# A two-branch attention: VectorE's share of the square moved before the second tile's absolute value, all lags one slot shorter

## The reference, cut to what matters

```python
S = jnp.einsum('bhnd,bhmd->bhnm', Q, K) / dh ** 0.5
W_tau = jax.nn.softmax(S, axis=-1)
W_sigma = 1.0 / ((1.0 + jnp.abs(S) / b_) ** 2 + t_ ** 2)
W_sigma = W_sigma / W_sigma.sum(axis=-1, keepdims=True)
tau = jnp.einsum('bhnm,bhmd->bhnd', W_tau, V)
sigma = jnp.einsum('bhnm,bhmd->bhnd', W_sigma, V)
f = 0.5 * tau + 0.5 * sigma
```

## Time and profile before

| | before |
|---|---|
| time, median of 3 runs | 2975.97 us (2975.95 to 2976.5) |
| time of the profiled execution | 2972.06 us |
| its span | 2970.4 us |
| busy: PE, DVE, ACT, POOL | 2445.4, 2491.1, 2234.4, 1992.1 us |
| granted TensorE clock, mean | 0.936 of full |

### The profile page before, as it was taken

The page is one execution under the profiler, slowest core; times in us unless marked ns, Lnnn a source line. Parts: engine busy times, 40 slices in busy tenths (PEclk is TensorE's granted clock), DMA queues, the critical chain, the costliest instruction groups (busy, mean ns, idle before and its releaser), DMA issues. The chain is left out here.

```text
span 2970.4 us, 60006 instructions
## 1 busy us (share of the span) xinstructions
PE 2445.4 (82%) x18487; PEld 1018.8 (34%) x18614; DVE 2491.1 (84%) x3983; ACT 2234.4 (75%) x2441; POOL 1992.1 (67%) x1236
## 2 busy tenths in 40 slices
PE   3755999998577994689999999999999999983898
PEld 2642333333474662122222222222222222222566
DVE  4666888885577657799999999999999999996765
ACT  4532777777364543499999999999999999993554
POOL 4510222222453651499999999999999999994465
PEclk9976999999687997699999999999999999997799
DMA  3222111000120002000000000000000000000000
GB/s 116 70 64 87 30 29 29 28 27 11 45 79 5 1 0 86 22 15 14 16 15 14 14 16 15 14 14 16 15 14 14 16 15 14 14 5 0 1 12 18
DMA packets 93504, 76.58 MB, mean 26 GB/s; under 512 B 32480, under 2 KB 73960, under 8 KB 93264
## 3 DMA queue, kind: packets, MB, share of 16 engines
q1 hardware_dynamic: 89104, 66.36, 7.8%
q0 software_dynamic: 4288, 8.82, 0.9%
HBM read 47.77 MB, written 24.42 MB: 24 GB/s over the span
## 5 line engine op out<-in xcount | busy, mean ns | idle before, releaser
L1761 POOL TENSOR_TENSOR a_sg<-a_sg,all_f0w 128x1632 f32<-128x1632 f32 x256 | 940.7, 3675 | 21.3
L1967 DVE TENSOR_REDUCE a_mx<-a_pm 128x1 f32<-128x1024 f32 x512 | 618.3, 1208 | 23.2 <-PE a_pm L1813 23.2
L1978 DVE TENSOR_SCALAR a_sg<-a_pa 128x1024 int32<-128x1024 int32 x512 | 614.9, 1201 | 3.8 <-PE a_pa L1813 3.8
L1894 ACT ACTIVATE a_pt<-a_pb 128x1024 f32<-128x1024 f32 x512 | 532.4, 1040 | 55.0 <-PE a_pb L1813 53.4
L1831 PE MATMUL a_po<-a_pt,a_Vh 128*32 128x512 f32 x2048 | 538.4, 604 | 15.0 <-ACT a_osb L1913 11.4
L1831 PE MATMUL a_po<-a_sg,a_Vh 128*32 128x512 f32 x2048 | 538.3, 604 | 0.0
L1758 POOL TENSOR_SCALAR all_f0w<-a_sg,a_parh 128x1632 f32<-128x1632 f32 x256 | 506.7, 1979 | 37.4 <-DVE a_sg L1978 37.3
L1903 ACT ACTIVATE a_sg<-a_sg,a_parh 128x2048 f32<-128x2048 f32 x256 | 517.0, 2020 | 0.0
L1907 ACT ACTIVATE a_sg<-a_sg 128x2048 f32<-128x2048 f32 x256 | 496.0, 1937 | 0.0
L1581 ACT ACTIVATE a_pt<-a_ring 128x1024 f32<-128x1024 f32 (+2 forms) x384 | 313.7, 846 | 164.4 <-PE a_ring L1508 161.2
L1653 DVE TENSOR_REDUCE a_mx<-a_ring 128x2 f32<-128x1024 f32 (+3 forms) x384 | 359.2, 955 | 85.1 <-PE a_ring L1491 66.1
(11 more groups left out here) (265 smaller groups left out, 4457.9 us busy)
## 6 DMA issues: line engine op xcount, KB each, us to landing
all_Q<-q_parts SPq DMA_DIRECT2D x256, 48.0 KB
all_K<-k_parts SPq DMA_DIRECT2D x256, 48.0 KB
k_parts<-p_parts SPq DMA_DIRECT2D x16, 384.0 KB, 2.6
e_recs<-routed_rows SPq DMA_DIRECT2D x70, 64.5 KB, 1.9
n_xn<-expert_rows SPq DMA_DIRECT2D x16, 256.0 KB, 4.2
all_Q<-a_rows SPq DMA_DIRECT2D x256, 2.0 KB
q_parts<-p_parts SPq DMA_DIRECT2D x16, 192.0 KB, 2.3
q_parts<-p_parts SPq DMA_DIRECT2D x8, 384.0 KB, 2.6
```

Source lines behind the costliest of these rows:

```text
L1761: nc.gpsimd.tensor_tensor(buf[:, :, 0:CUT], buf[:, :, 0:CUT], sums, ALU.mult)\
L1894: nc.scalar.activation(pt[(j - LT) % 4][:, i, :], pb[:], ACT.Exp, scale=SC)\
L1967: nc.vector.tensor_reduce(mx[:, (j // PER) % 2, t:t + 1], pm[:], AX.X, ALU.max)\
L1978: nc.vector.tensor_scalar(sg[(j - LS) % 4][:, i, :].bitcast(I32), pa[:].bitcast(I32), SIGN_OFF, None, ALU.bitwise_and).then_inc(abs_done, 1)
```

## The change

Four things change, all in `attend_both`:

- The DVE square works on columns 0 to 415 of the first tile alone (`CUT` = 13 * 1024 / 32 = 416), where it had 208 columns of each tile. GpSimd's share is what is left of the two tiles seen as one row of 2048: 1632 columns. Both shares are as large as before.
- The DVE square needs the abs of the first tile only, and stands between the second tile's maximum and the second tile's abs.
- The turning of the maxima moves from the second to the first half of an iteration, and both parts of `negated` run in that same iteration. `output` and the turning of `osb` are spread differently: the add into F (L1957 in the changed kernel) now stands just before the DVE square.
- All lags fall by one: `LS`, `LT`, `LE`, `LP` from 5, 7, 7, 8 to 4, 6, 6, 7. The distances between the square, the reciprocal and the weighing stay the same; the distance from the maxima to the softmax's scores falls by a slot.

```diff
--- before.py
+++ after.py
@@ -1673,9 +1673,9 @@
     SLOTS = HEADS * TT // 2
     PER = TT // 2
     UNROLL = PER * RING
-    LS, LT, LE, LP = 5, 7, 7, 8
+    LS, LT, LE, LP = 4, 6, 6, 7
     SC = DH ** -0.5
-    CUT = 51 * T // 64
+    CUT = 13 * T // 32
     WIDE = TT * (DH + 1)
     with ExitStack() as ctx:
         m = Mem(nc, ctx, tag)
@@ -1686,8 +1686,8 @@
         rows = m.sb("rows", [TT, MAX_PARTS, P], BF16)
         pt = [m.sb(f"pt{r}", [P, 2, T]) for r in range(4)]
         sg = [m.sb(f"sg{r}", [P, 2, T]) for r in range(4)]
-        shifted = [scratch[:, 4 * CUT * r:4 * CUT * (r + 1)].bitcast(F32).rearrange("p (i n) -> p i n", i=2)
-                   for r in range(2)]
+        REST = 2 * T - CUT
+        shifted = [scratch[:, 2 * REST * r:2 * REST * (r + 1)].bitcast(F32) for r in range(2)]
         osb = m.sb("osb", [P, CH])
         rz = m.sb("rz", [P, 4, 4])
         fw = m.sb("fw", [P, 4, 4, DH])
@@ -1730,7 +1730,7 @@
             with eng.Fori(1, SLOTS // UNROLL) as it:
                 for j in range(UNROLL):
                     body(it, j)
-            for j in range(LP + 4):
+            for j in range(LP + 5):
                 body(SLOTS // UNROLL, j)
 
         def some(x, least=1):
@@ -1747,7 +1747,8 @@
                     s = at(it, j, LS)
                     if s is None:
                         return
-                    buf, sums = sg[(j - LS) % 4], shifted[(j - LS) % 2]
+                    buf = sg[(j - LS) % 4][:].rearrange("p i n -> p (i n)")[:, CUT:]
+                    sums = shifted[(j - LS) % 2]
                     if some(s, 2):
                         pool.wait_ge(sq_pool, s - 1)
                     if (j - LS) % PER == 0:
@@ -1755,10 +1756,10 @@
                     pool.wait_ge(abs_done, 2 * s + 2)
                     pool.nop(nofuse=True)
                     b2 = parh[:, ring(j, LS), 0:1]
-                    nc.gpsimd.tensor_scalar(sums, buf[:, :, 0:CUT], b2, 1.0, ALU.add, ALU.mult)\
+                    nc.gpsimd.tensor_scalar(sums, buf, b2, 1.0, ALU.add, ALU.mult)\
                         .then_inc(shift_done, 1)
                     pool.wait_ge(shift_done, s + 1)
-                    nc.gpsimd.tensor_tensor(buf[:, :, 0:CUT], buf[:, :, 0:CUT], sums, ALU.mult)\
+                    nc.gpsimd.tensor_tensor(buf, buf, sums, ALU.mult)\
                         .then_inc(sq_pool, 1)
 
                 slots(pool, body)
@@ -1853,7 +1854,7 @@
                             if some(2 * ss + i):
                                 pe.wait_ge(abs_done, 2 * ss + i)
                             scores(pa, K[rs], Q[rs], 2 * ((j - LS) % PER) + i, 96, abs_mm)
-                        if i == 1 and j % PER == 0 and at(it, j, 1) is not None:
+                        if i == 0 and j % PER == 0 and at(it, j, 1) is not None:
 
                             h = head(it, j, 1)
                             pe.wait_ge(max_red, TT * h + TT)
@@ -1864,19 +1865,19 @@
                         sp_ = at(it, j, LP + 1 - i)
                         if sp_ is not None:
                             weigh(it, j, sp_, 1 - i)
-                    if (j - LP - 2) % PER == PER - 1 and at(it, j, LP + 2) is not None:
-
-                        h = head(it, j, LP + 2)
-                        pe.wait_ge(o_sb, h + 1)
-                        if isinstance(h, int) and h + 3 > HEADS:
-                            pe.wait_ge(rows_sb, HEADS)
-                            pe.wait_ge(f_done, h)
-                        else:
-                            pe.wait_ge(rows_sb, h + 3)
-                        for c in range(4):
-                            last = nc.tensor.transpose(ptr[:, c * P:(c + 1) * P], osb[:, c * P:(c + 1) * P],
-                                                       ident[:])
-                        last.then_inc(o_turned, 1)
+                        if i == 0 and (j - LP - 3) % PER == PER - 1 and at(it, j, LP + 3) is not None:
+
+                            h = head(it, j, LP + 3)
+                            pe.wait_ge(o_sb, h + 1)
+                            if isinstance(h, int) and h + 3 > HEADS:
+                                pe.wait_ge(rows_sb, HEADS)
+                                pe.wait_ge(f_done, h)
+                            else:
+                                pe.wait_ge(rows_sb, h + 3)
+                            for c in range(4):
+                                last = nc.tensor.transpose(ptr[:, c * P:(c + 1) * P], osb[:, c * P:(c + 1) * P],
+                                                           ident[:])
+                            last.then_inc(o_turned, 1)
 
                 slots(pe, body)
 
@@ -1967,26 +1968,24 @@
                             nc.vector.tensor_reduce(mx[:, (j // PER) % 2, t:t + 1], pm[:], AX.X, ALU.max)\
                                 .then_inc(max_red, 1)
                         if i == 0:
-                            negated(it, j, 1, 2)
-                            output(it, j, 0, LP + 3)
+                            output(it, j, 1, LP + 4)
                         else:
-                            output(it, j, 1, LP + 3)
+                            output(it, j, 2, LP + 4)
+                        if i == 1 and ss is not None:
+                            share = sg[(j - LS) % 4][:, 0, 0:CUT]
+                            dve.wait_ge(abs_done, 2 * ss + 1)
+                            if (j - LS) % PER == 0:
+                                dve.wait_ge(head_in[ring(j, LS)], HEAD_LOADS * rounds(it, j, LS))
+                            nc.vector.scalar_tensor_tensor(share, share, parh[:, ring(j, LS), 0:1], share,
+                                                           ALU.add, ALU.mult).then_inc(sq_dve, 1)
                         if ss is not None:
                             dve.wait_ge(abs_mm, 2 * ss + i + 1)
                             if some(ss, 4):
                                 dve.wait_ge(pv_done, 2 * (ss - 4) + i + 1)
                             nc.vector.tensor_scalar(sg[(j - LS) % 4][:, i, :].bitcast(I32), pa[:].bitcast(I32),
                                                     SIGN_OFF, None, ALU.bitwise_and).then_inc(abs_done, 1)
-                    if ss is not None:
-                        buf = sg[(j - LS) % 4]
-                        dve.wait_ge(abs_done, 2 * ss + 2)
-                        if (j - LS) % PER == 0:
-                            dve.wait_ge(head_in[ring(j, LS)], HEAD_LOADS * rounds(it, j, LS))
-                        nc.vector.scalar_tensor_tensor(buf[:, :, CUT:T], buf[:, :, CUT:T],
-                                                       parh[:, ring(j, LS), 0:1], buf[:, :, CUT:T],
-                                                       ALU.add, ALU.mult).then_inc(sq_dve, 1)
-                    negated(it, j, 0, 1)
-                    output(it, j, 2, LP + 3)
+                        negated(it, j, i, 1)
+                    output(it, j, 0, LP + 3)
 
                 slots(dve, body)
         m.clear_sems()
```

## The result

| | before | after |
|---|---|---|
| time, median of 5 runs | 2975.95 us (2971.5 to 2976.5) | 3341.33 us (3338.93 to 3342.76) |
| span of the profiled execution | 2970.4 us | 3337.2 us |
| busy: PE, DVE, ACT, POOL | 2445.4, 2491.1, 2234.4, 1992.1 us | 2560.4, 2778.0, 2259.7, 1904.1 us |
| granted TensorE clock, mean | 0.936 | 0.903 |

The ratio is 1.123, with a 95% interval of 1.1215 to 1.1245. The change makes the kernel 12% slower; 3342 us was forecast. The medians in this document are those of fast runs; one run of e7, 3260.27 us at a mean clock of 0.73, is left out.

A forecast was written before the change was run, and what follows sets the result against it. The prediction took GpSimd, running back to back at 5.70 us a slot, to bound the second attention. 359.6 + 13 - 4.7 - 2 = +366 us on 2972.06 gave 3338, as a median 3342 us; range 3300 to 3440, at 80%.

The forecast's parts named there:

- The lock: Second attention: GpSimd's multiply keeps DVE's square out, which ends some 0.45 us after it; a square keeps GpSimd's shift out.
- The closed cycle: Second attention: square waits for multiply, GpSimd then for the second abs; 7.11 us a slot for 5.70, 359.6 us more.
- The add ahead of the square: Add into F also waits for the multiply, delaying the square by up to 0.2 us in one slot of four: 13 us.
- The fill: Start of the second attention: shorter lags leave out one slot of maxima alone, -4.7 us.
- The last slots: Last four slots lack maxima, so the square may slip in ahead of the multiply: -2 us, within 0 to -5.
- The sum: All terms together: 359.6 + 13 - 4.7 - 2 = +366 us on the profiled execution's 2972.06.
- TensorE's clock: Second attention: TensorE, needing 5.14 us a slot, 72% of 7.16, was left at its granted clock of 1.00.
- Rival 3: TensorE's clock falls in the attention's longer gaps; for a third of it 265 us more, 3600 us; 5%.
- Rivals 1 and 2: DVE runs a slot ahead: 2971 us (6%), or 2958 us if square and shift don't exclude each other (4%).

The follow-up runs named there:

- e7: e1 with DVE's share of the square raised from 416 to 512 of 2048 columns; 2959.62 us, ratio 0.9946 to the kernel before.
- e4: Changed kernel, its order kept, with DVE's square and add into F each reading one of their two inputs from PSUM; 2951.49 us, ratio 0.992.
- e5: Changed kernel with GpSimd's multiply replaced by a second shift, so each GpSimd instruction reads one SBUF tensor; 2949.75 us in one run.
- e3: Kernel before with the change's shares and the DVE square ahead of the second abs; lags, turning and add as before; 3334.68 us, ratio 1.1208.
- e2: e1 with the add into F ahead of the second abs in one slot of four; 3046.54 us, ratio 1.0236.
- e1: Changed kernel with the DVE square put back behind the second abs and the add into F at the slot's end; 2968.59 us, ratio 0.9977.
- e8: Changed kernel with GpSimd waiting in the very first slot for the abs of two slots instead of one; 3340.34 us, ratio 1.123.

## Why the prediction was right

- *The lock.* Shown by e4, with e5 for the shift. The multiply keeps the square out. Whatever else the order costs doesn't reach the time: with the lock gone GpSimd still waits for an abs now and then (31.5 us in the 800), but ACT sets the pace.
- *The closed cycle.* The term was 7.11 us a slot; three slots in four take 7.13 us in the timeline, and e3 with the order alone has 7.13 on the mean. Its parts: the multiply's end to the abs 0.37 (2013.92 to 2014.29), abs 1.21, 0.17 to the shift, shift 1.62 for the 1.60 chosen between 1.50 and 1.97, hand-over 0.09, multiply 3.65. That some 0.35 us of the shift before (the prediction took 0.4) was DVE's square, and not its own work, shows in its median, now 1625 ns for 1970.
- *The add ahead of the square.* 13 us were forecast, 0.2 us a head. The slot with the add:

```profile
2001.23 1.62 POOL L1759 TENSOR_SCALAR all_f0w<-a_sg,a_parh 128x1632 f32<-128x1632 f32 x1 [1.76 <-DVE a_sg L1985]
...
2004.67 2.00 DVE L1957 TENSOR_TENSOR all_XNT<-a_fw 128x64 f32 x1
...
2006.59 0.64 DVE L1979 SCALAR_TENSOR_TENSOR a_sg<-a_sg,a_parh 128x416 f32<-128x416 f32 x1
...
2008.54 1.63 POOL L1759 TENSOR_SCALAR all_f0w<-a_sg,a_parh 128x1632 f32<-128x1632 f32 x1 [1.96 <-DVE a_sg L1985]
```

  It is 7.31 us long, 0.18 more than the others. e2 shows what the prediction left out: the same add would have cost 78 us in a kernel that is otherwise in the good order.
- *The fill.* -4.7 us were forecast. From the first maximum to the first shift it is 4.2 us less in the changed kernel and 4.8 us less in e1.
- *The last slots.* -2 us were forecast and none were won there. Without maxima a square begins 0.46 us after a multiply has begun (3022.86 against 3022.40) and takes 3.65 us. This term was wrong, within its bounds of 0 to -5.
- *The sum.* The cycle and the add were put at 359.6 + 13 = 372.6 us, and the shifts' starts show 373.1. That the totals then agree within 1 us (366 forecast, 366.8 between the spans) is in part luck: the 2 us of the last slots were not won, and 2.5 us came from what was in no term (the stage's earlier start 1.35, the last shift 0.35, the end 0.8).
- *TensorE's clock.* It was left at 1.00 and fell to 0.92 on the mean of the stage (row at the end): the step failed, the 74% of the earlier trace rows was no guide. Rival 3's price did not come with it, though. DVE waits 57 us for maxima's scores in the 1100 us above, and the time comes out of the square's wait:

```profile
2024.50 3.64 POOL L1762 TENSOR_TENSOR a_sg<-a_sg,all_f0w 128x1632 f32<-128x1632 f32 x1
...
2026.31 1.23 DVE L1968 TENSOR_REDUCE a_mx<-a_pm 128x1 f32<-128x1024 f32 x1 [1.24 <-PE a_pm L1814]
...
2027.45 1.14 DVE L1979 SCALAR_TENSOR_TENSOR a_sg<-a_sg,a_parh 128x416 f32<-128x416 f32 x1
...
2028.52 1.21 DVE L1985 TENSOR_SCALAR a_sg<-a_pa 128x1024 int32<-128x1024 int32 x1
...
2029.90 1.62 POOL L1759 TENSOR_SCALAR all_f0w<-a_sg,a_parh 128x1632 f32<-128x1632 f32 x1 [1.75 <-DVE a_sg L1985]
```

  The maximum is 1.24 us late, the square 1.14 us long for 2.63, and the shift still starts 1.76 us after the multiply's end.
- *Rivals 1 and 2.* The prediction argued that nothing would bring DVE ahead, and in the changed kernel nothing does. e8 gave the rivals the head start that they need, once and at the start of the stage, and it was lost within five slots. That such a state may not last is a reason that the prediction did not have; with the lower clock of those slots e8 doesn't show it for the whole stage.

## What to carry to other kernels

A short VectorE instruction with two inputs in SBUF can wait for a long GpSimd one that reads SBUF, and its place in the queue decides what that costs: last in the slot it cost 0.35 us of each shift, ahead of what GpSimd waits for 1.4 us a slot. Look for instructions whose duration varies and whose end keeps a fixed distance from the end of an instruction elsewhere; such a wait shows as busy time, in no list of waits. And count every instruction with two inputs in SBUF, however short: where it is shut out, one of 64 columns waits for the multiply's end as one of 416 does.

## What was not expected of the hardware

The lock works at both ends of a hand-over. A square that begins 0.10 us before a multiply makes the multiply wait (4.08 us for 3.65 in e8); one that begins at the same time to 0.01 us (3029.61 in the changed kernel, 4.14 us), or 0.07 us into it (3023.73 against 3023.66 in e3, 4.05 us), waits to its end. In the kernel before the square that was let go won over GpSimd's shift in every slot (no shift took less than 1954 ns), although the trace shows the shift as started. TensorE's granted clock was lower on the mean of the stage although PE was busier than in the last 35 us of the earlier trace rows, which had 74% and 1.00. The window of the stage after the change (us; PE, PEld, DVE, ACT, POOL busy; PEclk; DMA share; GB/s):

```profile
1220.00:3050.00 1830.00, 1428.93 (x7277) 369.38 (x7407) 1732.82 (x1579) 1465.66 (x1081) 1347.26 (x511) 0.92 0.04 11
```

PE is busy 78% of it, at a mean clock of 0.92: some matmuls ran at 1.2 GHz and longer (a pair for the maxima took 1.06 us at 2025.21 and 0.61 us at 2028.72), so its share rose over the 72% of the forecast. The busy share alone does not tell the clock.
